# Layer 1 of a convolution front end: two neighbouring positions from five products in place of six

## The chip, the cores and the metric

The kernel runs on one core of one Trainium2 chip. The metric is the device time of one execution in microseconds (us). TensorE (PE in the rows) multiplies, VectorE (DVE), ScalarE (ACT) and GpSimd (POOL) do the elementwise work, SyncE (SP) issues most transfers. Each engine runs its own instructions in order and waits on semaphores for the others.

## The reference, cut to what matters

Eight signals of 120,000 samples go through seven convolutions of 128 channels, each followed by a LayerNorm over the channels and an exact GELU. Four later stages work on the 8 x 374 tokens that are left; the change doesn't touch them.

```python
CONVS = [(128, 10, 5)] + [(128, 3, 2)] * 4 + [(128, 2, 2)] * 2      # channels, taps, stride
for w, g, b, s in zip(conv_ws, ln_gs, ln_bs, strides):
    h = _conv1d(h, w, s)                      # 'VALID', no bias
    h = _fp32_layernorm(swap(h), g, b)        # over the 128 channels
    h = jax.nn.gelu(swap(h), approximate=False)
```

Layer 1 has three taps and stride 2: output position m is w0 x[2m] + w1 x[2m+1] + w2 x[2m+2], where each w is a 128 x 128 matrix. Its outputs m and m+1 both use x[2m+2]: one with w2, the other with w0.

## The kernel before

The samples run through `stream` in 47 chunks (`CHUNKS`, loop variable `j`). A chunk holds 32 positions of layer 0 for 128 stretches of signal, which lie across the partitions. A chunk has eight groups g0 to g7, given by `GROUPS`: g0 to g3 are the four groups of layer 1, g4 is layer 4 (two tiles), g5 is layer 3, g6 and g7 are layer 2. A group is four tiles of 128 x 128 (one bank of PSUM, `psY`), and a tile is three products, one for each tap (`products`, L290). So a layer-1 group is 12 products.

Each group goes round the engines:

- TensorE: `conv` (it waits until the group three before has been normalised, since there are three banks), then the transposes (L299) of the group two before (`LAG = 2`).
- ScalarE: `square` (L349) into `sq`, later `gelu` (L367) of the group two before.
- VectorE: `stats` (the sum L392 into `ss`, and L395, which scales it and adds EPS into `var`), other work of the chunk, then `normalise` (L403).
- GpSimd: `root` (L466), a power of -0.5 over 4 columns, between `stats` and `normalise` of the same group.

Beside that, each chunk makes layer 0 of the next: `window_transposes` and `gram_product` (L323, L329), `patch_squares` (L422, in g0), `patch_stats` (L428 and L430, in g1), `split_patches` (part 0 in g6: L440 to L450; part 1 in g7: L453 to L456), `patch_root` (L472, on GpSimd behind the roots of g2 to g5), `patch_transposes` (L311; the two halves behind g2 and g3 on TensorE) with `copy_patches` (L411; on VectorE between `stats` and `normalise` of g2 and g3), and eight products `layer0` (L339) into `psL`, whose GELU is L383. The second half of `patch_transposes` waits for the copy of the first.

From chunk 8 on, the layers 5 and 6 and the first token stages of a signal (a "side chain" of 36 steps, `pe_chain`, `act_chain`, `dve_chain`, `pool_chain`) are laid over six chunks. `STEP_AT` says behind which of the 48 groups each step goes; -1 is a group without one. On GpSimd, steps 0, 3 and 6 are small roots, 9, 14 and 28 too (L964, L969), 16 and 17 are two additions or products of 125 x 576 (L979, L984), and steps 0, 1 and 3 also issue an indirect DMA each (L989, `pool_scatter`). In the first five chunks VectorE computes tables between the groups instead (`ssm_tables`, L1528 to L1530).

## Time and profile before

| | before |
|---|---|
| median of 3 runs | 2412.24 us (2410.5 to 2412.98) |
| profiled execution | 2409.08 us, span 2407.2 us |
| TensorE busy | 2186.4 us, 91% |
| VectorE busy | 1359.7 us, 56% |
| ScalarE busy | 1141.2 us, 47% |
| GpSimd busy | 861.3 us, 36% |
| products of layers 1 to 4 (L290) | 1045.5 us busy, 8508 rows |

A float32 product of 128 x 128 stands in the profile as two rows (two passes), so 24 rows are the 12 products of a group. The loop over the chunks takes from about 60 us to about 1425 us. One turn of it can be measured by the start of VectorE's copy L416, which comes once in a chunk, ahead of the sum of g6.

### The profile page before, as it was taken

The numbers are of one execution on the slowest core, as the hardware profiler recorded it, in microseconds if no ns is written. First come the engines' busy times: TensorE is split into PE (matmuls) and PEld (weight loads), VectorE is DVE, ScalarE is ACT, GpSimd is POOL, SyncE is SP. The second block draws the span as 40 slices with busy tenths as digits, with TensorE's granted clock in tenths as the row PEclk, the third lists the DMA queues.
The fourth block names the chain that finished last, engine by engine and source line by source line (L and its number), as shares of the span: only waits on it lengthen the run. The fifth ranks groups of instructions, "written<-read, shape, count | busy, mean of one in ns | idle before, by whom it ended". The sixth has DMA issues, their size and how long they took to land. (4 is left out here: it accounts for less than half of the span.)

```text
span 2407.2 us, 45725 instructions
## 1 busy us (share of the span) xinstructions
PE 2186.4 (91%) x16643; PEld 2013.0 (84%) x16643; DVE 1359.7 (56%) x3616; ACT 1141.2 (47%) x2203; POOL 861.3 (36%) x760
## 2 busy tenths in 40 slices
PE   2999999999999999999999995978697899969988
PEld 1999999999999999999999884978465567759988
DVE  4676667667667667667667652422486365542222
ACT  1655565555555565565555541322243465542320
POOL 4444555555555555554554531101330000000000
PEclk9999999999999999999999996999799899989989
DMA  5700000000000000000000202656000010109966
GB/s 159 238 4 4 5 4 4 6 8 4 8 6 4 8 6 4 8 6 4 9 4 1 65 1 73 186 162 181 20 20 1 26 52 39 52 39 326 332 202 223
DMA packets 101336, 150.65 MB, mean 63 GB/s; under 512 B 14692, under 2 KB 79118, under 8 KB 100364
## 3 DMA queue, kind: packets, MB, share of 16 engines
q1 hardware_dynamic: 77580, 118.36, 15.6%
q10 hardware_dynamic: 17984, 20.30, 2.6%
q0 software_dynamic: 5568, 9.27, 1.3%
q8 instruction: 128, 2.10, 0.4%
q14 instruction: 76, 0.62, 0.1%
HBM read 102.32 MB, written 45.50 MB: 61 GB/s over the span
## 5 line engine op out<-in xcount | busy, mean ns | idle before, releaser
L290 PE MATMUL banks<-t_wt,t_l 128*128 128x128 f32 x8508 | 1045.5, 277 | 4.1 <-ACT t_l L367 2.9
L290 PEld LDWEIGHTS banks<-t_wt,t_l 128*128 128x128 f32 x8508 | 1014.9, 193 | 19.5 <-ACT t_l L367 4.1
L466 POOL TENSOR_TENSOR t_rstd<-t_var,t_minus_half 128x4 f32<-128x4 f32 (+1 forms) x379 | 367.0, 968 | 640.1 <-DVE t_var L395 638.7
L349 ACT ACTIVATE t_sq<-banks 128x512 f32<-128x512 f32 (+1 forms) x379 | 216.0, 570 | 523.2 <-PE banks L290 521.3
L403 DVE TENSOR_TENSOR t_yn<-banks,t_rstd 128x512 f32<-128x512 f32 (+1 forms) x379 | 249.1, 657 | 366.2 <-POOL t_rstd L466 364.4
L383 ACT ACTIVATE t_l<-banks,t_cols 128x512 f32<-128x512 f32 x376 | 286.6, 777 | 79.4 <-PE banks L339 76.6
L472 POOL TENSOR_TENSOR t_zrstd<-t_zvar,t_minus_half 128x8 f32<-128x8 f32 x188 | 307.6, 1637 | 25.4 <-DVE t_zvar L430 25.4
L392 DVE TENSOR_REDUCE t_ss<-t_sq 128x4 f32<-128x512 f32 (+1 forms) x379 | 244.7, 646 | 88.8 <-ACT t_sq L349 83.3
L367 ACT ACTIVATE t_l<-banks,t_cols 128x512 f32<-128x512 f32 (+1 forms) x381 | 284.8, 748 | 12.6 <-PE banks L299 7.8
L299 PE MATMUL banks<-t_ident,t_yn 128*128 128x128 f32 x1426 | 220.1, 274 | 13.1 <-DVE t_yn L403 11.9
L299 PEld LDWEIGHTS banks<-t_ident,t_yn 128*128 128x128 f32 x1426 | 173.4, 142 | 27.2 <-DVE t_yn L403 14.9
L339 PE MATMUL banks<-t_p60T,t_w 120*128 120x512 bf16 x376 | 137.4, 386 | 1.9 <-ACT t_l L383 1.8
L1478 POOL TENSOR_TENSOR t_nrstd<-t_nvar,t_minus_half 125x3 f32<-125x3 f32 x24 | 20.7, 863 | 270.1 <-DVE t_nvar L1472 270.1
L1110 ACT ACTIVATE t_G<-banks,t_b1T 128x128 f32<-128x128 f32 x162 | 47.7, 365 | 122.4 <-PE banks L1062 122.0
L2220 DVE TENSOR_SCALAR t_a<-t_H,t_late 128x128 f32 (+1 forms) x128 | 39.3, 340 | 114.9 <-PE banks L2153 106.8
L2152 PE MATMUL banks<-t_a,t_w 128*128 128x128 f32 x384 | 75.7, 279 | 6.5 <-DMA t_w1x<-in_w1x 6.5
L2283 PE MATMUL banks<-t_yb,t_ectb 128*125 128x192 f32 (+1 forms) x384 | 66.5, 336 | 14.0 <-DVE t_yb L2258 10.3
L2283 PEld LDWEIGHTS banks<-t_yb,t_ectb 128*125 128x125 f32 (+1 forms) x384 | 64.9, 194 | 15.6 <-DVE t_yb L2258 10.6
L2086 DVE TENSOR_REDUCE t_ltm<-banks 128x1 f32<-128x374 f32 x64 | 34.8, 544 | 75.5 <-PE banks L1866 75.4
L2153 PE MATMUL banks<-t_a,t_w1x 65*128 65x128 f32 x384 | 75.5, 278 | 0.0
L2160 PE MATMUL banks<-t_w,t_eg 128*128 128x192 f32 x384 | 73.3, 327 | 1.3 <-ACT t_eg L2179 1.3
L395 DVE TENSOR_SCALAR t_var<-t_ss 128x4 f32<-128x4 f32 (+1 forms) x379 | 65.3, 172 | 13.1
(324 smaller groups left out, 3305.5 us busy)
## 6 DMA issues: line engine op xcount, KB each, us to landing
t_w<-in_w SPq DMA_DIRECT2D x64, 480.0 KB
t_w<-in_w SPq DMA_DIRECT2D x27, 576.0 KB, 5.7
ect<-t_ECT SPq DMA_DIRECT2D x16, 750.0 KB, 3.2
t_l<-in_w1a SPq DMA_DIRECT2D x27, 384.0 KB, 5.3
sorted_by_expert<-t_h SPq DMA_DIRECT2D x4, 2400.0 KB, 11.0
routed_by_expert<-t_h SPq DMA_DIRECT2D x4, 2400.0 KB, 17.4
t_ectb<-ect ACTq DMA_DIRECT2D x5, 1500.0 KB, 7.9
t_w1x<-in_w1x SPq DMA_DIRECT2D x64, 97.5 KB
```

The lines of the kernel that those rows point to most:

```text
L290: mm = pe.matmul(psY[bank][:, t * C:(t + 1) * C], src[:, at:at + P], T["wt"][:, 3 * (layer - 1) + k, :], start=(k == 0), stop=(k == 2))
L299: mm = pe.transpose(psT[:, t * P:(t + 1) * P], T["yn"][:, par, t * C:(t + 1) * C], T["ident"][:, :])
L339: pe.matmul(psL[i % 2][:, :], T["w60"][:, slot, :], p60T[:, 4 * q:4 * q + 4, :].rearrange("r a p -> r (a p)"), start=True, stop=True).then ...
L349: act.activation(T["sq"][:, par, 0:n], psY[bank][:, 0:n], ACT.Square).then_inc(S["squared"], 1)
L367: act.activation(dst, psT[:, 0:n].rearrange("c (t p) -> c t p", p=P), ACT.Gelu, bias=T["cols"][:, 8 + layer:9 + layer], scale=T["cols"][:, ...
L383: act.activation(view(T["l0"][:, :], [[2 * BLOCK, 4], [1, P]], block_at(0, 8 * q + slot)), psL[i % 2][:, :].rearrange("c (a p) -> c a p", ...
L392: dve.reduce_sum(T["ss"][:, par, 0:n], T["sq"][:, par, 0:n * C].rearrange("p (t c) -> p t c", c=C), axis=AX.X)\
L403: dve.tensor_tensor(T["yn"][:, par, 0:n * C].rearrange("p (t c) -> p t c", c=C), psY[bank][:, 0:n * C].rearrange("p (t c) -> p t c", c=C), ...
L466: pool.tensor_tensor(T["rstd"][:, par, 0:n], T["var"][:, par, 0:n], T["minus_half"][:, 0:n], ALU.pow)\
L472: pool.tensor_tensor(T["zrstd"][:, s], T["zvar"][:, s], T["minus_half"][:, 0:POS // 4], ALU.pow)\
L2152: pe.matmul(o, T["w12"][:, r, c * P:(c + 1) * P], T["a1"][:, r % RING, :], start=True, stop=False)
L2283: mm = pe.matmul(pO[k % 2][0:n, 0:D], T["ectb"][:, b % MIX_RING, c, t * TOK:t * TOK + n], T["yb"][:, b % MIX_RING, c, :], start=(c == 0), ...
```

## The change

Layer 1 (g0 to g3) is computed as follows. For the pair of outputs m and m+1, which share x[2m+2], one product with `wsum` = w0 + w2 is made of the shared input (the shared product). Each of the two outputs then takes its middle tap as before, and one product of a difference: x[2m] - x[2m+2] with w0, x[2m+4] - x[2m+2] with w2. The shared product is added to both. A group has 2 + 4 + 4 = 10 products.

- TensorE: `pair_products` puts the two shared products into `psL` ahead of the wait for the bank, then the eight others into `psY`.
- GpSimd: `differences` writes 128 x 512 differences into `dif` for each of the four groups: one instruction for three of them, three instructions for the first. They stand ahead of the roots of g6, g7, g0 and g1.
- ScalarE: `read_shared` copies the 128 x 256 shared products from PSUM to `shared`.
- VectorE: `add_shared` adds them to the bank in PSUM. It stands ahead of `normalise` of the group before (of g7 for g0), and waits for the products of its own group. `square` of layer 1 now waits for it.
- VectorE's L395 is gone from the groups: the square is scaled by 1/sqrt(C) on ScalarE, and EPS is a 129th column of `sq`.
- The two halves of `patch_transposes` and `copy_patches` stand one group earlier (g1 and g2), and `STEP_AT` is another table.
- To make room, `v` holds two signals in place of eight, with a wait for the indirect DMA two signals back.

```diff
     def conv(pe, j, g):
-        layer = GROUPS[g][0]
-        pe.wait_ge(S["normed"], count(j, g) - BANKS)
-        if layer == 1:
-            if g == 0:
-                pe.wait_ge(S["l0_ready"], 8 * (j + 1))
+        if g == 0:
+            pe.wait_ge(S["l0_ready"], 8 * (j + 1))
+        if g < WG:
+            pair_products(pe, j, g)
         else:
...
+    def pair_products(pe, j, g):
+        _, half, bank, par, _, _ = event(j, g)
+        if sums(j, g) > 2:
+            pe.wait_ge(S["shared_read"], sums(j, g) - 2)
+        for p in range(2):
+            at = tap(1, out_blocks(1, half)[2 * p], 2)
+            mm = pe.matmul(psL[par][:, p * C:(p + 1) * C], T["l0"][:, at:at + P], T["wsum"][:, :], start=True, stop=True)
+        mm.then_inc(S["shared_done"], 1)
+        pe.wait_ge(S["normed"], count(j, g) - BANKS)
+        pe.wait_ge(S["dif_ready"], 4 * j + (2, 2, 3, 4)[g])
+        for t, m in enumerate(out_blocks(1, half)):
+            o, at = psY[bank][:, t * C:(t + 1) * C], tap(1, m, 1)
+            pe.matmul(o, T["l0"][:, at:at + P], T["wt"][:, 1, :], start=True, stop=False)
+            mm = pe.matmul(o, T["dif"][:, half, t * P:(t + 1) * P], T["wt"][:, t % 2 * 2, :], start=False, stop=True)
+        mm.then_inc(S["conv_done"], 1)
...
-        dve.reduce_sum(T["ss"][:, par, 0:n], T["sq"][:, par, 0:n * C].rearrange("p (t c) -> p t c", c=C), axis=AX.X)\
-            .then_inc(S["summed"], 1)
-        dve.wait_ge(S["summed"], number)
-        dve.tensor_scalar(T["var"][:, par, 0:n], T["ss"][:, par, 0:n], 1.0 / C, EPS, ALU.mult, ALU.add)\
-            .then_inc(S["var_ready"], 1)
+        dve.reduce_sum(T["var"][:, par, 0:n], T["sq"][:, par, 0:n, :], axis=AX.X).then_inc(S["summed"], 1)
+
+    def read_shared(act, j, g):
+        par = event(j, g)[3]
+        act.wait_ge(S["shared_done"], sums(j, g))
+        if sums(j, g) > 2:
+            act.wait_ge(S["added"], sums(j, g) - 2)
+        act.activation(T["shared"][:, par, :], psL[par][:, 0:2 * C], ACT.Copy).then_inc(S["shared_read"], 1)
+
+    def add_shared(dve, j, g):
+        _, _, bank, par, number, _ = event(j, g)
+        shared = view(T["shared"][:, par, :], [[C, 2], [0, 2], [1, C]])
+        y = psY[bank].rearrange("p (a b c) -> p a b c", a=2, b=2)
+        dve.wait_ge(S["shared_read"], sums(j, g))
+        dve.wait_ge(S["conv_done"], number)
+        dve.tensor_tensor(y, y, shared, ALU.add).then_inc(S["added"], 1)
...
+    def differences(pool, j, half):
...
+        pool.wait_ge(S["conv_done"], count(j - 1, 3))
+        pool.wait_ge(S["l0_ready"], 8 * j + (7, 3, 5, 7)[half])
+        if half == 0:
+            at = block_at(0, POS - 2) - 1
+            pool.tensor_tensor(out[:, 0, :], l0[:, at:at + P], even(1, 1)[:, 0, :], ALU.subtract)
+            pool.tensor_tensor(out[:, 1, :], even(2, 1)[:, 0, :], even(1, 1)[:, 0, :], ALU.subtract)
...
+        pool.tensor_tensor(o, pairs, middle, ALU.subtract).then_inc(S["dif_ready"], 1)
...
-    STEP_AT = [-1, 0, 1, -1, 2, 3, 4, -1, 5, 6, 7, 8, 9, 10, 11, 12, -1, 13, 14, 15, -1, 16, 17, 18, -1, 19, 20, 21, 22, 23, -1, 24, 25,
-               -1, 26, 27, 28, 29, 30, 31, -1, 32, 33, -1, 34, 35, -1, -1]
+    STEP_AT = [0, -1, 1, -1, 2, 3, 4, -1, 5, 6, 7, -1, 8, 9, 10, -1, 11, 12, -1, 13, 14, 15, 16, 17, 18, -1, 19, 20, 21, 22, 23, 24, 25,
+               -1, 26, -1, 27, 28, 29, -1, 30, 31, 32, 33, -1, 34, 35, -1]
...
                 for g in range(NG):
+                    if g < 2:
+                        differences(pool, j, g + 2)
+                    if g >= 6 and j + 1 < CHUNKS:
+                        differences(pool, j + 1, 7 - g)
                     root(pool, event(j, g))
```

VectorE from the sum of g7 to the normalise of g0, before (L392 and L395 `stats`, L403 `normalise`, L453 to L456 the second part of `split_patches`, L422 `patch_squares`):

```order
L392 TENSOR_REDUCE t_ss<-t_sq 128x4
L395 TENSOR_SCALAR t_var<-t_ss 128x4
L403 TENSOR_TENSOR t_yn<-banks,t_rstd 128x512
L453 TENSOR_TENSOR t_p<-t_rest,t_p 128x32x10
L455 COPY t_p<-t_p 128x32x10 x2
L456 COPY t_p<-t_p 128x32x10
```

The same place after (L430 `stats`, L445 `add_shared`, L452 `normalise`, L502 to L505 `split_patches`, L471 `patch_squares`), on to the normalise of g0:

```order
L430 TENSOR_REDUCE t_var<-t_sq 128x4
L445 TENSOR_TENSOR banks<-banks,t_shared 128x512
L452 TENSOR_TENSOR t_yn<-banks,t_rstd 128x512
L502 TENSOR_TENSOR t_p<-t_rest,t_p 128x32x10
L504 COPY t_p<-t_p 128x32x10 x2
L505 COPY t_p<-t_p 128x32x10
L430 TENSOR_REDUCE t_var<-t_sq 128x4
L471 TENSOR_TENSOR t_zz<-banks,t_xs 128x320
L445 TENSOR_TENSOR banks<-banks,t_shared 128x512
L452 TENSOR_TENSOR t_yn<-banks,t_rstd 128x512
```

L395 has gone, and the addition for the next group has come between the sum and the normalise.

GpSimd from the last `patch_root` (L540) of a chunk to g2 of the next, after (L515 `root`, L527, L528 and L535 `differences`). Before, only the five roots stand between the two L472:

```order
L540 TENSOR_TENSOR t_zrstd<-t_zvar,t_minus_half 128x8
L535 TENSOR_TENSOR t_dif<-t_l 128x512
L515 TENSOR_TENSOR t_rstd<-t_var,t_minus_half 128x4
L527 TENSOR_TENSOR t_dif<-t_l 128x128
L528 TENSOR_TENSOR t_dif<-t_l 128x128
L535 TENSOR_TENSOR t_dif<-t_l 128x256
L515 TENSOR_TENSOR t_rstd<-t_var,t_minus_half 128x4
L535 TENSOR_TENSOR t_dif<-t_l 128x512
L515 TENSOR_TENSOR t_rstd<-t_var,t_minus_half 128x4
L535 TENSOR_TENSOR t_dif<-t_l 128x512
L515 TENSOR_TENSOR t_rstd<-t_var,t_minus_half 128x4 x2
L540 TENSOR_TENSOR t_zrstd<-t_zvar,t_minus_half 128x8
```

The roots of g6, g7, g0 and g1 now each stand behind the differences of a later group.

## Rows read from the trace of the kernel before

**Rows 1.** Busy time by engine: a chunk without side chain, six with it.

```profile
core 0: us, PE busy (x) PEld busy (x) DVE busy (x) ACT busy (x) POOL busy (x), PEclk, DMA share, GB/s
...
227.99:254.83 26.84, 26.84 (x243) 26.30 (x242) 16.37 (x40) 16.18 (x28) 14.13 (x13) 1.00 0.02 4
...
518.72:695.50 176.78, 175.95 (x1545) 170.64 (x1545) 119.36 (x307) 102.15 (x180) 96.55 (x84) 1.00 0.02 6
```

**Rows 2.** Who TensorE waited for, 60 to 1430 us: sum, times, longest.

```profile
PE banks L525 <- DVE t_yn L718: 7.5, 4, 2.5
PE banks L311 <- DVE t_p60T L411: 6.8, 5, 1.9
```

**Rows 3.** Timeline of TensorE over g0 to g1 of chunk 5: start, length.

```profile
207.35 2.84 PE L290 MATMUL banks<-t_wt,t_l 128*128 128x128 f32 x24
210.03 0.60 PE L299 MATMUL banks<-t_ident,t_yn 128*128 128x128 f32 x4
210.47 2.84 PE L290 MATMUL banks<-t_wt,t_l 128*128 128x128 f32 x24
```

**Rows 4.** Timeline of VectorE: the copy L416 of chunks 1 and 2.

```profile
114.10 0.42 DVE L416 COPY t_xT<-banks 85x256 f32<-85x256 f32 x1
...
142.90 0.42 DVE L416 COPY t_xT<-banks 85x256 f32<-85x256 f32 x1
```

**Rows 5.** Timeline of VectorE: g1 of a chunk, to the sum of g2.

```profile
213.91 0.68 DVE L392 TENSOR_REDUCE t_ss<-t_sq 128x4 f32<-128x512 f32 x1
214.62 0.17 DVE L395 TENSOR_SCALAR t_var<-t_ss 128x4 f32<-128x4 f32 x1
215.91 0.69 DVE L403 TENSOR_TENSOR t_yn<-banks,t_rstd 128x512 f32<-128x512 f32 x1 [1.12 <-POOL t_rstd L466]
216.52 0.48 DVE L428 TENSOR_REDUCE t_zs<-t_zz 128x32 f32<-128x320 f32 x1
...
217.12 0.68 DVE L392 TENSOR_REDUCE t_ss<-t_sq 128x4 f32<-128x512 f32 x1
```

**Rows 6.** Timeline of GpSimd, g2 and g3 of the same chunk.

```profile
218.08 1.01 POOL L466 TENSOR_TENSOR t_rstd<-t_var,t_minus_half 128x4 f32<-128x4 f32 x1 [2.21 <-DVE t_var L395]
219.06 1.64 POOL L472 TENSOR_TENSOR t_zrstd<-t_zvar,t_minus_half 128x8 f32<-128x8 f32 x1
220.69 1.01 POOL L466 TENSOR_TENSOR t_rstd<-t_var,t_minus_half 128x4 f32<-128x4 f32 x1
```

**Rows 7.** Timeline of VectorE: `patch_squares`, and both parts of `split_patches` with what follows.

```profile
204.20 0.48 DVE L440 TENSOR_TENSOR t_scaled<-t_xs,t_zrstd 128x320 f32<-128x320 f32 x1
...
205.85 0.28 DVE L1529 TENSOR_SCALAR t_late<-t_cosT,t_sv 128x118 f32<-128x118 f32 x1
...
209.16 0.48 DVE L453 TENSOR_TENSOR t_p<-t_rest,t_p 128x320 bf16<-128x320 f32 x1
...
210.26 0.16 DVE L1528 TENSOR_TENSOR t_sv<-t_sv 128x1 f32<-128x1 f32 x1 [0.16 <-DVE t_p L456]
...
212.09 0.48 DVE L422 TENSOR_TENSOR t_zz<-banks,t_xs 128x320 f32<-128x320 f32 x1
```

**Rows 8.** Timeline of GpSimd: step 17 of the side chain, ahead of chunk 23.

```profile
726.48 1.41 POOL L984 TENSOR_TENSOR t_h<-t_h,t_late 125x576 f32<-125x576 f32 x1
```

**Rows 9.** Timeline of VectorE at the same time: the first operation of `split_patches`.

```profile
727.15 1.08 DVE L440 TENSOR_TENSOR t_scaled<-t_xs,t_zrstd 128x320 f32<-128x320 f32 x1
```

**Rows 10.** Timeline of GpSimd: step 0 with its indirect DMA, chunk 20.

```profile
651.88 0.85 POOL L964 TENSOR_TENSOR t_rstd<-t_var,t_minus_half 125x3 f32<-125x3 f32 x1 [2.07 <-DVE t_var L708]
652.94 1.28 POOL L989 DMA_INDIRECT sorted_by_expert<-t_v,t_row  x1 [0.21 <-issue]
654.25 1.05 POOL L466 TENSOR_TENSOR t_rstd<-t_var,t_minus_half 128x4 f32<-128x4 f32 x1
```

**Rows 11.** Timeline of VectorE around that step 0.

```profile
651.71 0.68 DVE L392 TENSOR_REDUCE t_ss<-t_sq 128x4 f32<-128x512 f32 x1
...
655.33 0.69 DVE L403 TENSOR_TENSOR t_yn<-banks,t_rstd 128x512 f32<-128x512 f32 x1 [2.14 <-POOL t_rstd L466]
```

More of the change, by code:

```diff
@@ L52 @@
 BANKS = 3
+WG = 4
 XS_RING = 4
@@ L202, in _ @@
                 .then_inc(S["wt_centred"], 1)
+            dve.wait_ge(S["wt_centred"], 1)
+            dve.wait_ge(S["w0_split"], 1)
+            dve.tensor_tensor(T["wsum"][:, :], T["wt"][:, 0, :], T["wt"][:, 2, :], ALU.add)
         @block.tensor
@@ L254, in event, with sums, sums_behind @@
         return GROUPS[g] + ((NG * j + g) % BANKS, g % 2, count(j, g), P * j)
+    def sums(j, g):
+        return WG * j + g + 1
+    def sums_behind(j, g):
+        return (j, g + 1) if g + 1 < WG else (j + 1, 0) if g + 1 == NG and j + 1 < CHUNKS else None
     END = (CHUNKS + 1) * NG
@@ L335, in layer0 @@
             pe.wait_ge(S["patch_copied"], 2 * c + i // 4 + 1)
-        if not isinstance(c, int) or 8 * c + i >= 2:
+        if c >= 1 and i < 2:
+            pe.wait_ge(S["shared_read"], sums(c - 1, 2 + i))
+        if 8 * c + i >= 2:
             pe.wait_ge(S["l0_ready"], 8 * c + i - 1)
@@ L344, in square @@
     def square(act, e):
-        layer, _, bank, par, number, _ = e
+        layer, half, bank, par, number, _ = e
         n = tiles(layer) * C
-        act.wait_ge(S["conv_done"], number)
+        if layer == 1:
+            act.wait_ge(S["added"], sums(number // NG - 1, half))
+        else:
+            act.wait_ge(S["conv_done"], number)
         act.wait_ge(S["summed"], number - 2)
-        act.activation(T["sq"][:, par, 0:n], psY[bank][:, 0:n], ACT.Square).then_inc(S["squared"], 1)
+        act.activation(T["sq"][:, par, 0:tiles(layer), 0:C], psY[bank][:, 0:n].rearrange("p (t c) -> p t c", c=C), ACT.Square,
+                       scale=C ** -0.5).then_inc(S["squared"], 1)
     def gelu(act, e, carry=None):
@@ L467, in root @@
             .then_inc(S["rstd_ready"], 1)
+    def differences(pool, j, half):
+        l0 = T["l0"]
+        even = lambda i, n: view(l0[:, :], [[4 * BLOCK, n], [1, P]], block_at(0, 8 * half - 2 + 2 * i))
+        out = T["dif"][:, half, :].rearrange("p (t c) -> p t c", c=P)
+        pool.wait_ge(S["conv_done"], count(j - 1, 3))
[4 more added lines that the diff above has]
+            pool.tensor_tensor(out[:, 1, :], even(2, 1)[:, 0, :], even(1, 1)[:, 0, :], ALU.subtract)
+            pairs, o = view(l0[:, :], [[4 * BLOCK, 2], [1, P]], block_at(0, 2)), out[:, 2:4, :]
+            middle = view(l0[:, :], [[0, 2], [1, P]], block_at(0, 4))
+        else:
+            pairs = view(l0[:, :], [[4 * BLOCK, 2], [4 * BLOCK, 2], [1, P]], block_at(0, 8 * half - 2))
+            middle = view(l0[:, :], [[4 * BLOCK, 2], [0, 2], [1, P]], block_at(0, 8 * half))
+            o = out.rearrange("p (a b) c -> p a b c", a=2)
+        pool.tensor_tensor(o, pairs, middle, ALU.subtract).then_inc(S["dif_ready"], 1)
     def patch_root(pool, c, part):
@@ L1315, in _ @@
                         gram_product(pe, j + 3)
+                    if g == 1 and j + 1 < CHUNKS:
+                        patch_transposes(pe, j + 1, 0)
                     if g == 2 and j + 1 < CHUNKS:
-                        patch_transposes(pe, j + 1, 0)
-                    if g == 3 and j + 1 < CHUNKS:
                         patch_transposes(pe, j + 1, 1)
@@ L1344, in _ @@
                 gelu0(act, 0, i)
+            read_shared(act, 0, 0)
             for j in range(CHUNKS):
@@ L1359, in _ @@
                     act_chain(act, *chain_at(j, g))
+                    if sums_behind(j, g):
+                        read_shared(act, *sums_behind(j, g))
             gelu(act, event(CHUNKS - 1, 6))
@@ L1396, in _ @@
                 split_patches(dve, c, 1)
+            add_shared(dve, 0, 0)
             for j in range(CHUNKS):
@@ L1403, in _ @@
                         patch_squares(dve, j + 2)
+                    if g == 1 and j + 1 < CHUNKS:
+                        copy_patches(dve, j + 1, 0)
                     if g == 2 and j + 1 < CHUNKS:
-                        copy_patches(dve, j + 1, 0)
-                    if g == 3 and j + 1 < CHUNKS:
                         copy_patches(dve, j + 1, 1)
+                    if sums_behind(j, g):
+                        add_shared(dve, *sums_behind(j, g))
                     normalise(dve, event(j, g))
@@ L1441, in _ @@
                     patch_root(pool, c, part)
+            differences(pool, 0, 1)
+            differences(pool, 0, 0)
             for j in range(CHUNKS):
                 for g in range(NG):
+                    if g < 2:
+                        differences(pool, j, g + 2)
+                    if g >= 6 and j + 1 < CHUNKS:
+                        differences(pool, j + 1, 7 - g)
                     root(pool, event(j, g))
@@ L2421, in program @@
                         sl("w0parts", [TAPS0, 3, C], BF16)
[L2422 removed]
+                        sl("wsum", [P, C])
+                        T["w0rest"] = T["wsum"][0:TAPS0, :]
                         sl("w0c", [P, TAPS0])
@@ L2436, in program @@
                         sl("p60T", [2 * ROWS, PAIRS, P], BF16)
+                        sl("dif", [P, 4, 4 * P])
+                        sl("shared", [P, 2, 2 * C])
                         sl("l0", [P, BLOCK * BLOCKS[0]])
```

32 lines of the change are left out of this document (19 added, 13 removed).

## The prediction

> **What bounds the kernel now.** I read the busy time by engine first, then who TensorE waits for. In the loop over the chunks TensorE is the bound: a chunk without side chain takes 26.84 us and TensorE is busy for all of it, six chunks with side chain take 176.78 us and it is busy for 175.95 [rows 1]. Its waits in the loop come to a handful, 6.8 us for the copied patches and 7.5 for step 1 of the side chain [rows 2]. VectorE is busy for 61% of the plain chunk and GpSimd for 53%, 68% and 55% in the six. That looks like ample room. It isn't, because the two take turns: a group's sum is followed by a root on GpSimd, and the normalise queued behind it on VectorE waits for that root. The first sum starts at 213.91 and the normalise at 215.91, 2.00 us of which VectorE works 0.85; the next operation starts 0.61 later [rows 5]. So I add up the turn of VectorE and GpSimd in order, as if TensorE were always ready, and compare it with TensorE's own sum. I count from the sum of g7 to that of the next g7.
>
> **The turn before.** g7: 2.61, and 1.10 for the second part of the split (209.16 to 210.26) [rows 5, 7]. g0: 2.61. g1: 2.61 and 0.60 for the patch sums (216.52 to 217.12) [rows 5]. g2: 2.61. That is 12.14 to the sum of g3; the copies and squares between sum and normalise hide under the root. The root starts 0.96 after the sum (2.00 less 1.04 for the root and its signal), so at 13.10. From here GpSimd is the path: root 0.98, patch root 1.63, root, and so on [rows 6]; the root of g4 has two columns and takes about 0.66. Root 3, patch root, root 4, patch root, root 5 end at 18.94. The normalise of g5, the window copy and the sum of g6 with its signal give 20.9; root 21.9, normalise 22.6, first part of the split 1.65 (204.20 to 205.85) [rows 7]: 24.2 us. TensorE needs 26.84. The margin is 2.6 us.
>
> As a test of the method: the first five chunks carry the tables of VectorE, about 0.7 us behind most groups, and take 28.8 us (114.10 to 142.90) [rows 4]. The turn plus tables gives 24.2 + 4.6, and TensorE waits. So the turn can be the bound, and is there.
>
> **TensorE after.** Twelve products take 210.03 - 207.35 = 2.68 us, 0.223 each [rows 3]. Ten instead of twelve in four groups: 8 x 0.223 = 1.79 us less, so 25.05 in a plain chunk and 29.46 - 1.79 = 27.67 in one with side chain. Over 47 chunks this is 84 us, what the change could give at most.
>
> **The turn after, part by part.**
> - L395 is gone: its result came 0.25 later than the sum's (214.62 to the root) and the root now follows the sum by some 0.77. Sum to normalise is 1.81, a group 2.42. This saves 0.19 in each group on VectorE's path.
> - add_shared isn't in the trace. It reads PSUM and SBUF over 512 columns and writes PSUM; bounds are 0.48 (L422, 320 columns, the same sources) [rows 7] and 0.69 (L403, 512 columns) [rows 5]. I take the latter, 0.61 to the next operation. In g7 it hides under the root; in g0 with L422 it just fits (1.74 of 1.81); in g1 and g2 with the copy it makes 1.90, so 0.09 each.
> - read_shared is 256 columns on ScalarE, which is busy for 16.18 of 26.84 [rows 1], and has two thirds of the products' time to do it. Nothing.
> - The differences. The nearest row is 125 x 576 on GpSimd, 1.41 us [rows 8]: 512 columns at 2.45 ns are 1.25. The group in three instructions lies between 1.25 and 2.0; I take 1.45. The ones ahead of the root of g6 stand directly in GpSimd's path: +1.25, of which 0.35 fits into the time in which it waited for the sum. The others fit between roots.
> - Their second cost is on VectorE. In the trace one operation of `split_patches` runs while L984 does. L984 lasts from 726.48 to 727.89; L440 starts at 727.15 and takes 1.08 in place of 0.48, ending 0.34 after it [rows 7 to 9]; so in six of six side chains. The differences of the next g0 start right behind the root of g6, exactly as L984 did, so L440 loses about 0.6 in every chunk. Those of g2 start behind the root of g7 and hold L453 for about 0.4. The bounds for both are 0 and 1.5, all of the differences that outlasts the normalise (1.45 - 0.61 and 1.25 - 0.61). I take 1.0, since that is how L440 fared.
>
> The Trainium skill, page SBUF — State Buffer, section "Who interferes with whom", says that a VectorE instruction with two SBUF inputs and a GpSimd instruction that reads SBUF exclude each other for the whole instruction, and whoever starts second waits it out. The trace agrees for L440 (it ended 0.34 after L984). Copies and casts, it says, can take the shared ports too; by that rule the rest of the split would be held as well and the cost would be 1.5 in place of 1.0, 24 us over the loop.
>
> Sum: g7 1.81 + 0.61 + 1.10 + 0.4 = 3.93; g0 2.42; g1 1.90 + 0.61 + 0.60 = 3.11; g2 2.51; sum of g3 at 11.97. Its root would start at 12.75 and GpSimd is free at 12.8. Root, patch root, root, patch root, root, patch root end at 20.3, the differences at 21.5, root 6 at 22.5, normalise 23.2, split 1.65 + 0.6: **25.45 us**. The turn was 2.6 us shorter than TensorE's sum; now it is 0.4 longer. A plain chunk becomes 25.45 in place of 26.84.
>
> **The side chain on top.** It adds (119.36 / 6) - 16.37 = 3.5 us of VectorE and 2.0 of GpSimd to a chunk [rows 1], and on TensorE 2.6. Before, a margin of 2.6 and TensorE's own 2.6 took that up. Now, for six chunks, by the new table: steps of VectorE behind g6, g7, g0, g1 and g2, where nothing hides them, 11.9 us (0.92 for a pair of 374-column products, 1.7 for step 35, and so on). Steps of GpSimd in its path 9.6: step 0 stands at g0, and its small root 0.85 and its indirect DMA 1.28 come ahead of the differences and of the root of g1. In the trace this already stretched 2.00 to 655.33 - 651.71 = 3.62 [rows 10, 11]; now the differences are added, about 2.9 more than the 1.90. Steps 1 and 3 cost 1.3 and 2.1, steps 9, 14 and 28 some 1.1 each. Steps 16, 17 and 25 meet the port as L440 did: 1.6. What spills over in g3 and g4: 2.1. Round trips over TensorE when its part of a step is behind g2: 2.1. Together 27.3 us, 4.55 a chunk. The turn is then 30.0 us, against 27.67 for TensorE and 29.46 measured before. So six chunks take 180.0 in place of 176.78.
>
> **Total.** Five batches of six at +3.3: +16.5. The first batch has no indirect DMAs (4.1 less): -2. The last three chunks have a step behind every group: +3. Five table chunks: 25.45 + 4.6 against 28.8, +6. Three plain ones: 3 x -1.4 = -4. The first differences stand between the last GELU of layer 0 and the first products: +1.5, bounds 0 and 3. Nothing changes behind the loop. Sum +21, which makes 2430 us of the profiled execution's 2409.08. That execution was 3.2 us under the median of the runs, so the median should go from 2412 to about 2433 us.
>
> **Rivals.**
> 1. *The turn is overlapped after all*, since TensorE may be two groups ahead, and TensorE stays the bound. For it: 61% busy. Against it: the table chunks. It gives 2412 - 84 + some 10 us of stalls = 2338. It decides if the turn with side chain is under 27.7.
> 2. *No port cost*: the differences are short, or VectorE slips between them. The turn loses 1.0 a chunk, and 1.6 in a batch: -47 - 10, so 2376. Against it: L440 in six of six.
> 3. *Slower still*: each stall of TensorE comes back. The second patch transposes, behind g2, wait for a copy that now stands behind the sum of g1; TensorE reaches it with nothing to spare, and what follows (0.45 of transposes, 2.23 of products, add_shared) reaches VectorE late. With 0.5 a chunk for the port at its upper bound and 0.3 for these trips: 47 x 0.8 = +38 on the forecast, so 2471.
> 4. *The side chain hides better*: a quarter of its 27.3 us falls into waits that I count as none, among them VectorE's wait for the root in g3 to g5. -6.8 x 6.5 = -44, so 2389. For it: TensorE's waits before are far below what single late groups would suggest [rows 2]. Against it: 3.62 in place of 2.00 [rows 11].
>
> **How the numbers follow.** Forecast 0.45, rival 1 0.12, rival 2 0.12, rival 3 0.17, rival 4 0.14. I predict 2433 us. The range leaves out rival 1 and takes in the others, with the upper bound of the port cost: 2368 to 2472. A measurement of this kernel can tell about 0.2% (5 us). Rivals 1, 2 and 4 are faster, and the forecast loses 0.05 to no change: faster 0.36, same 0.06, slower 0.58.
>
> **What would show it.** TensorE's idle time in the loop goes from some 20 us to over 100, waiting for L460 (the copied patches) and L452 (the normalise). The copy L465 comes every 25.4 to 26 us in chunks 5 to 7 and every 30 on average later. L489 takes about 1.08 in every chunk. The differences take 1.2 to 1.3 us. Chunks with step 0 are the longest. If the copies come every 27.7 us I am wrong about the turn; if L489 takes 0.48, about the port.

## The result, and the profile after

The changed kernel takes **2502.12 us** (median; 2497.45 to 2504.8) against 2412.51 (2410.5 to 2412.98) for the kernel before on the same chip: a ratio of 1.0377, 95% interval 1.0362 to 1.0391. The prediction was 2433 with a range of 2368 to 2472. Slower was right; the 90 us are four times the 21 that were summed up.

Section 1 of the page after (busy time of each engine):

```profile
PE 2152.1 (86%) x15891; PEld 1959.3 (78%) x15891; DVE 1453.5 (58%) x3426; ACT 1193.7 (48%) x2391; POOL 1116.5 (45%) x1043
```

TensorE was busy for 2186.4 us before. It has lost only 34 us of work, GpSimd has gained 255 and VectorE 94, and no engine is near full. One round of VectorE and GpSimd through a chunk's eight groups is the turn of the forecast; the part of it from the sum of one group to that of the next is called a trip here. By the start of the copy that comes once in a chunk (L416 before, L465 after), the 96 us of span lie so:

| stretch | before | after | more | forecast |
|---|---|---|---|---|
| to the fourth of these copies | 84.42 | 86.93 | 2.5 | 1.5 |
| four chunks with tables | 116.8 | 120.5 | 3.7 | 6 (for five) |
| three plain chunks | 80.4 | 82.8 | 2.4 | -4 |
| six chunks, first batch | 178.3 | 186.5 | 8.2 | -2 |
| five batches of six | 884.1 | 943.3 | 59.2 | 16.5 |
| the rest | 1063.2 | 1083.0 | 19.8 | 3 |

The five batches hold most of it, but for its length the worst place is the last three chunks, which stand in "the rest": from the sum of g7 of chunk 43 to that of chunk 46 it is 116.5 us after and 97.2 before. Behind the loop nothing is lost. Of the three plain chunks the first takes 29.11 us (26.73 before), the two others 26.82 and 26.83, as before.

Who TensorE waits for after, 60 to 1500 us (sum, times, longest). L343 is `patch_transposes`, L373 `layer0`, L306 and L307 the products of layer 1 in `pair_products`; L471 is `patch_squares`, L421 the GELU of layer 0, L535 `differences`. It answers to [rows 2]:

```profile
PE banks L343 <- DVE t_zz L471: 56.5, 37, 2.8
PE banks L373 <- ACT t_l L421: 40.9, 44, 2.4
PE banks L306 <- POOL t_dif L535: 30.2, 36, 3.1
```

The same question for VectorE. L452 is `normalise`, L515 `root`, L445 `add_shared`:

```profile
DVE t_yn L452 <- POOL t_rstd L515: 272.9, 222, 3.1
DVE banks L445 <- PE banks L307: 92.3, 63, 7.1
DVE t_var L430 <- ACT t_sq L386: 42.7, 39, 2.7
```

So TensorE, which waited for almost nothing [rows 2], waits 128 us in these three rows, for three different things. VectorE in turn waits 92 us for TensorE: the addition stands in the queue before the products it needs are made. Not all of that is new. Before, VectorE already waited for TensorE's products by way of ScalarE's square, and the last two rows above (135 us) stand against this one, of the kernel before over the same 60 to 1500 us:

```profile
DVE t_ss L392 <- ACT t_sq L349: 83.3, 83, 8.6
```

The windows of the plain chunk, of six chunks with side chain (forecast: 180.0), and of all five batches, with the columns of [rows 1]:

```profile
236.58:263.40 26.82, 25.44 (x227) 24.57 (x226) 18.08 (x35) 17.22 (x33) 19.54 (x19) 1.00 0.02 5
853.82:1043.04 189.22, 170.55 (x1452) 162.63 (x1451) 131.94 (x282) 108.80 (x204) 129.27 (x120) 0.99 0.02 6
476.70:1420.05 943.35, 849.41 (x7243) 809.07 (x7242) 659.62 (x1408) 544.04 (x1015) 646.50 (x596) 0.99 0.02 5
```

In this plain chunk TensorE's work fell nearly as forecast (to 25.44; forecast 25.05), and the chunk took as long as before.

**One turn, row by row.** VectorE from the sum of g7 (269.29) to the sum of g3 (282.06). L430 is the sum, L502 to L505 the second part of `split_patches`, L460 `copy_patches`:

```profile
269.29 0.68 DVE L430 TENSOR_REDUCE t_var<-t_sq 128x4 f32<-128x516 f32 x1
270.75 0.70 DVE L445 TENSOR_TENSOR banks<-banks,t_shared 128x512 f32<-128x512 f32 x1 [0.78 <-PE banks L307]
271.36 0.68 DVE L452 TENSOR_TENSOR t_yn<-banks,t_rstd 128x512 f32<-128x512 f32 x1
...
273.27 0.69 DVE L430 TENSOR_REDUCE t_var<-t_sq 128x4 f32<-128x516 f32 x1 [0.16 <-DVE t_p L505]
273.87 0.48 DVE L471 TENSOR_TENSOR t_zz<-banks,t_xs 128x320 f32<-128x320 f32 x1
274.27 0.69 DVE L445 TENSOR_TENSOR banks<-banks,t_shared 128x512 f32<-128x512 f32 x1
275.08 0.69 DVE L452 TENSOR_TENSOR t_yn<-banks,t_rstd 128x512 f32<-128x512 f32 x1
275.68 0.68 DVE L430 TENSOR_REDUCE t_var<-t_sq 128x4 f32<-128x516 f32 x1
276.28 0.68 DVE L460 COPY t_p60T<-banks 120x1024 bf16<-120x1024 bf16 x1
277.52 0.70 DVE L445 TENSOR_TENSOR banks<-banks,t_shared 128x512 f32<-128x512 f32 x1 [0.56 <-PE banks L307]
278.13 0.68 DVE L452 TENSOR_TENSOR t_yn<-banks,t_rstd 128x512 f32<-128x512 f32 x1
...
279.33 0.68 DVE L430 TENSOR_REDUCE t_var<-t_sq 128x4 f32<-128x516 f32 x1
...
282.06 0.69 DVE L430 TENSOR_REDUCE t_var<-t_sq 128x4 f32<-128x516 f32 x1
```

GpSimd and TensorE at the same time:

```profile
276.44 1.01 POOL L515 TENSOR_TENSOR t_rstd<-t_var,t_minus_half 128x4 f32<-128x4 f32 x1 [0.16 <-DVE t_var L430]
```
```profile
273.15 0.60 PE L331 MATMUL banks<-t_ident,t_yn 128*128 128x128 f32 x4
274.50 0.63 PE L343 MATMUL banks<-t_identb,t_p 128*120 128x128 bf16 x8 [0.75 <-DVE t_zz L471]
274.96 0.66 PE L300 MATMUL banks<-t_wsum,t_l 128*128 128x128 f32 x4
...
277.03 0.39 PE L307 MATMUL banks<-t_wt,t_dif 128*128 128x128 f32 x2
```

From g7 to g0 it took 3.98 us (forecast 3.93), in part by luck: the addition waited 0.78 for its products and put the normalise 2.07 behind the sum in place of 1.81, and the split lost less than was forecast. From g0 to g1 it took 2.41 (2.42). From g1 to g2 it took 3.65 where the forecast had 3.11, and this is why: TensorE came to the patch transposes at 273.75, waited 0.75 for the squares of g0 (273.87 on VectorE), and so finished the products of g2 late, at about 277.4. The addition waited for them 0.56, to 277.52. The root of g1 was ready at 277.45, but its normalise stands behind the addition and ran at 278.13, 0.68 late. A late VectorE makes TensorE late, and through the addition TensorE makes VectorE late: the forecast left the second out.

There is a second place. Behind the sum of g3 the forecast has the roots and patch roots of g3, g4 and g5 back to back. The sum of g5 waited for its square, which waits for products, and GpSimd stood idle before the root of g5:

```profile
287.81 0.69 DVE L430 TENSOR_REDUCE t_var<-t_sq 128x4 f32<-128x516 f32 x1 [1.25 <-ACT t_sq L386]
```
```profile
288.58 1.01 POOL L515 TENSOR_TENSOR t_rstd<-t_var,t_minus_half 128x4 f32<-128x4 f32 x1 [0.88 <-DVE t_var L430]
```

**The trips on the mean.** From the start of one sum to that of the next, mean of the 30 chunks of the five batches, us, in the kernels before and after and in five of the runs below:

| trip | before | after | no differences | no addition | neither | transposes back | squares first |
|---|---|---|---|---|---|---|---|
| g6 to g7 | 4.59 | 6.09 | 4.98 | 6.25 | 5.21 | 6.07 | 6.08 |
| g7 to g0 | 4.12 | 4.36 | 3.85 | 4.34 | 3.78 | 4.36 | 4.77 |
| g0 to g1 | 2.90 | 2.93 | 2.92 | 2.93 | 2.85 | 2.93 | 2.92 |
| g1 to g2 | 3.84 | 4.49 | 4.38 | 3.79 | 3.54 | 3.82 | 3.94 |
| g2 to g3 | 3.81 | 3.66 | 3.65 | 3.34 | 3.31 | 3.48 | 3.67 |
| g3 to g6 | 10.20 | 9.94 | 10.04 | 9.93 | 9.94 | 9.96 | 9.95 |

Against the kernel before, the chunk is longer in two places: from g6 to g7 (1.50), where the differences stand ahead of the root, and from g1 to g2 (0.65).

### The profile page after: what moved, and what is told of

It is laid out like the page before. It is cut to its first block and busy times, and to the rows that moved or that the text cites. A ratio compares the mean times of both kernels' runs of the same rounds, so it can differ in the third digit from the quotient of the medians.

```text
span 2503.0 us, 45303 instructions
## 1 busy us (share of the span) xinstructions
PE 2152.1 (86%) x15891; PEld 1959.3 (78%) x15891; DVE 1453.5 (58%) x3426; ACT 1193.7 (48%) x2391; POOL 1116.5 (45%) x1043
## 5 line engine op out<-in xcount | busy, mean ns | idle before, releaser
L515 POOL TENSOR_TENSOR t_rstd<-t_var,t_minus_half 128x4 f32<-128x4 f32 (+1 forms) x379 | 367.4, 969 | 466.0 <-DVE t_var L430 465.3
L322 PE MATMUL banks<-t_wt,t_l 128*128 128x128 f32 x3996 | 509.4, 278 | 2.9 <-ACT t_l L405 2.9
L322 PEld LDWEIGHTS banks<-t_wt,t_l 128*128 128x128 f32 x3996 | 495.8, 195 | 15.6 <-ACT t_l L405 4.0
L452 DVE TENSOR_TENSOR t_yn<-banks,t_rstd 128x512 f32<-128x512 f32 (+1 forms) x379 | 248.3, 655 | 290.4 <-POOL t_rstd L515 283.1
L306 PE MATMUL banks<-t_wt,t_l 128*128 128x128 f32 x1504 | 303.0, 284 | 33.2 <-POOL t_dif L535 33.1
L540 POOL TENSOR_TENSOR t_zrstd<-t_zvar,t_minus_half 128x8 f32<-128x8 f32 x188 | 307.7, 1638 | 25.4 <-DVE t_zvar L479 25.4
L421 ACT ACTIVATE t_l<-banks,t_cols 128x512 f32<-128x512 f32 x376 | 288.1, 781 | 62.8 <-PE banks L373 59.6
L307 PE MATMUL banks<-t_wt,t_dif 128*128 128x128 f32 x1504 | 300.0, 282 | 0.0
L430 DVE TENSOR_REDUCE t_var<-t_sq 128x4 f32<-128x516 f32 (+1 forms) x379 | 246.2, 650 | 74.2 <-ACT t_sq L386 64.1
L306 PEld LDWEIGHTS banks<-t_wt,t_l 128*128 128x128 f32 x1504 | 237.5, 199 | 39.5 <-issue 39.3
L307 PEld LDWEIGHTS banks<-t_wt,t_dif 128*128 128x128 f32 x1504 | 237.3, 199 | 0.0
L535 POOL TENSOR_TENSOR t_dif<-t_l 128x512 f32<-128x512 f32 (+1 forms) x188 | 224.8, 1196 | 2.5 <-ACT t_l L421 2.1
L445 DVE TENSOR_TENSOR banks<-banks,t_shared 128x512 f32<-128x512 f32 x188 | 130.3, 693 | 107.7 <-PE banks L307 103.2
L373 PE MATMUL banks<-t_p60T,t_w 120*128 120x512 bf16 x376 | 138.2, 388 | 42.0 <-ACT t_l L421 41.9
L300 PE MATMUL banks<-t_wsum,t_l 128*128 128x128 f32 x752 | 122.7, 287 | 1.2 <-ACT t_l L421 1.2
L343 PE MATMUL banks<-t_identb,t_p 128*120 128x128 bf16 x752 | 61.1, 226 | 61.8 <-DVE t_zz L471 57.2
L343 PEld LDWEIGHTS banks<-t_identb,t_p 128*120 128x120 bf16 x752 | 53.2, 138 | 73.9 <-issue 73.2
```

Of the source, the lines that this page charges most:

```text
L306: pe.matmul(o, T["l0"][:, at:at + P], T["wt"][:, 1, :], start=True, stop=False)
L307: mm = pe.matmul(o, T["dif"][:, half, t * P:(t + 1) * P], T["wt"][:, t % 2 * 2, :], start=False, stop=True)
L322: mm = pe.matmul(psY[bank][:, t * C:(t + 1) * C], src[:, at:at + P], T["wt"][:, 3 * (layer - 1) + k, :], start=(k == 0), stop=(k == 2))
L421: act.activation(view(T["l0"][:, :], [[2 * BLOCK, 4], [1, P]], block_at(0, 8 * q + slot)), psL[i % 2][:, :].rearrange("c (a p) -> c a p", ...
L430: dve.reduce_sum(T["var"][:, par, 0:n], T["sq"][:, par, 0:n, :], axis=AX.X).then_inc(S["summed"], 1)
L452: dve.tensor_tensor(T["yn"][:, par, 0:n * C].rearrange("p (t c) -> p t c", c=C), psY[bank][:, 0:n * C].rearrange("p (t c) -> p t c", c=C), ...
```

## The experiments

All were run beside the kernel before; the time is the median, the ratio is against that kernel (its medians in these runs: 2407.2 to 2410.4), and differences of under some 5 us are not told apart. "Five batches" is the stretch of the table above (943.3 after, 884.1 before).

**1. The differences, the addition, both.** In the first edit the subtractions are left out and `dif` holds a constant. The outputs are then not the reference's, nor are they wherever a part of the pair products' arithmetic is left out below.

```diff
...
-        pool.tensor_tensor(o, pairs, middle, ALU.subtract).then_inc(S["dif_ready"], 1)
+        pool.nop().then_inc(S["dif_ready"], 1)
```

> The changed kernel without the subtractions on GpSimd: the buffer of differences keeps a constant, the waits stay. Left out: 4 differences a chunk (1.27 us each). Theory B/C: the time falls by far more than a difference's own place in the order, to 2420 or less, since 5.6 us a chunk of GpSimd time, the port and TensorE's 30 us of waits for them go. Theory A: only the 30 us of waits for the differences go, 2465 to 2475.

Measured: 2425.5 us, ratio 1.0066 (1.0049 to 1.0082); five batches 894.3. The differences cost 77 us, between the two cases of the expectation (2420 or less, and 2465 to 2475). The forecast's terms for them were 0.9 a chunk in GpSimd's path and 1.0 for the port, 47 x 1.9 = 89.

How much of it is the port? Here each difference gives way to powers over six columns, on as little data as a root, one for each group:

```diff
+        pool.tensor_tensor(T["dif"][:, half, 0:6], T["dif"][:, half, 8:14], T["minus_half"][:, 0:6],
+                           ALU.pow).then_inc(S["dif_ready"], 1)
```

> The changed kernel with one power over 6 columns (about 1.3 us on GpSimd, hardly any operand traffic) in place of each group's differences. It keeps GpSimd's time and order and takes away the reading of 512 columns. If VectorE's loss at the shared port matters: 25 to 50 us less than 2502. If GpSimd's time alone matters: within 15 us of 2502 (a little less, since the first group's three subtractions take 1.8 us and the power 1.3).

Measured: 2469.24 us, ratio 1.0249 (1.0229 to 1.0269). 33 us are gone though GpSimd is still taken (a power takes 1.34 us, a difference 1.28, the group in three instructions 1.76; in all GpSimd works 9 us less), and the remaining 44 go when its time is free too. The groups of `split_patches` show where the 33 are. Busy time and mean ns, of after (L502 the add of part 1, L494 the first cast, L489 the first product):

```profile
L502 DVE TENSOR_TENSOR t_p<-t_rest,t_p 128x320 bf16<-128x320 f32 x47 | 44.8, 954 | 0.1
L494 DVE CAST t_p<-t_scaled 128x320 bf16<-128x320 f32 x47 | 31.4, 668 | 1.6
L489 DVE TENSOR_TENSOR t_scaled<-t_xs,t_zrstd 128x320 f32<-128x320 f32 x47 | 27.1, 577 | 6.7 <-POOL t_zrstd L540 6.6
```

and of this experiment (L503, L495, L490 are the same three):

```profile
L503 DVE TENSOR_TENSOR t_p<-t_rest,t_p 128x320 bf16<-128x320 f32 x47 | 22.7, 482 | 0.1
L495 DVE CAST t_p<-t_scaled 128x320 bf16<-128x320 f32 x47 | 15.4, 327 | 1.6
L490 DVE TENSOR_TENSOR t_scaled<-t_xs,t_zrstd 128x320 f32<-128x320 f32 x47 | 26.3, 560 | 6.7 <-POOL t_zrstd L531 6.6
```

The three are 38.9 us longer beside the subtractions, 0.83 a chunk. The forecast had 1.0, with 0.6 on L489, and 1.5 as the upper bound. It fell on the cast: L489 started between two of the short subtractions of g0 and ran in 0.50, and the cast behind it was held by the third. Rows of GpSimd and of VectorE:

```profile
266.54 0.41 POOL L527 TENSOR_TENSOR t_dif<-t_l 128x128 f32<-128x128 f32 x1
266.91 0.46 POOL L528 TENSOR_TENSOR t_dif<-t_l 128x128 f32<-128x128 f32 x1
267.32 0.98 POOL L535 TENSOR_TENSOR t_dif<-t_l 128x256 f32<-128x256 f32 x1
```
```profile
267.21 0.50 DVE L489 TENSOR_TENSOR t_scaled<-t_xs,t_zrstd 128x320 f32<-128x320 f32 x1
267.75 0.74 DVE L494 CAST t_p<-t_scaled 128x320 bf16<-128x320 f32 x1
268.52 0.49 DVE L496 TENSOR_TENSOR t_rest<-t_scaled,t_p 128x320 f32<-128x320 f32 x1
```

The Trainium skill, page SBUF — State Buffer, section "Who interferes with whom", says that casts can take the shared ports as well. The trace agrees: this cast, with one input in SBUF, takes 0.33 us without subtractions beside it and 0.67 with them.

Next, `read_shared` and `add_shared` are left out, and the square waits for the products again:

```diff
-                        add_shared(dve, *sums_behind(j, g))
...
-            act.wait_ge(S["added"], sums(number // NG - 1, half))
+            act.wait_ge(S["conv_done"], number)
```

> The changed kernel without read_shared and add_shared: the shared product is computed and not added, and the square of layer 1 waits for its own products, as before. If the new link (square behind the addition, addition ahead of the normalise) sets the time: 60 us less or more, 2440 or below. If GpSimd's differences and the moved transposes do: within 25 us of 2502.

Measured: 2445.35 us, ratio 1.0149 (1.0132 to 1.0166); five batches 917.6. The addition, with the copy and the waits that belong to it, costs 57 us, again between the two cases (2440 or below, and within 25 of 2502). What the copy on ScalarE has of it was not measured alone. The forecast let it hide under the roots but for 0.09 in g1 and in g2, 8 us in all. The table of trips says where it is: nothing in g7 and g0, 0.70 from g1 to g2 and 0.32 from g2 to g3. The last three chunks alone fall from 116.5 to 100.8 us (without the differences to 105.2). And both left out:

> The changed kernel with neither the subtractions on GpSimd nor the copy and the addition of the shared product; what is left are ten products for twelve, the moved patch transposes, the new step table and the sum without L395. Left out: the differences' values and the shared product's addition. Removing the differences alone gave -77 us, the addition alone -57. If the two costs add: 2502 - 134 = 2368. If they share one path (VectorE waits behind GpSimd either way), 2390 to 2420. If TensorE is the bound again: 2330 to 2345.

Measured: 2360.55 us, ratio 0.9795 (0.9777 to 0.9813). 2502 less 77 and less 57 is 2368, so the two costs nearly add up. What fewer products and the single sum bring with the new order of work is some 50 us against the kernel before (2409.95 beside this run), and the two helpers cost 142.

**2. Is it TensorE's side or the turn?** Here the order, the table and the single sum of after stay, but layer 1 has its twelve products back, no addition, and the differences are computed and not used:

> The changed kernel's order, table and sum, with the 12 products of before and neither copy nor addition of the shared product; GpSimd still computes the differences, and nobody uses them. It does the reference's work. If the differences hide as long as TensorE has its full load: at most 15 us above the kernel before with L395 taken out (2390), so 2390 to 2405. If they stretch the turn whatever TensorE does: 2440 or more.

Measured: 2479.85 us, ratio 1.029 (1.0264 to 1.0316). This run does the reference's work, and the pair products are not needed for a loss. Against the kernel before with one sum (next, 2390.27) it is 90 us. Of that the order and the table may be some 15 (2360.55 to 2345.67, below), though with both helpers in place they cost 55 (experiment 3), so the subtractions' own share is not settled by the times. By trips it stands where they are: g6 to g7 takes 6.25 us here, 5.21 with the same order and no subtractions, 4.26 in the kernel before with one sum. GpSimd's subtractions make the loop longer though no product reads them.

The other way round: the kernel before with one part of the change alone, the scaled square and EPS as the 129th column, so that L395 goes:

```diff
...
-        dve.tensor_scalar(T["var"][:, par, 0:n], T["ss"][:, par, 0:n], 1.0 / C, EPS, ALU.mult, ALU.add)\
-            .then_inc(S["var_ready"], 1)
+        dve.reduce_sum(T["var"][:, par, 0:n], T["sq"][:, par, 0:n, :], axis=AX.X).then_inc(S["summed"], 1)
```

> The kernel before, with only L395 taken out of the groups (the square scaled, EPS as a 129th column). My reading: the turn of VectorE and GpSimd is 1.5 us shorter, which helps only the five table chunks and the few waits: 2 to 10 us less than 2410. Rival (L395 never on the path): no difference.

Measured: **2390.27 us**, ratio 0.992 (0.9906 to 0.9934), 20 us under the kernel before beside it. It computes what the reference does, and beats both kernels. I expected 2 to 10 us. Of its 18.8 us of span, 5.8 are in the four chunks with tables (116.84 to 111.07), where the turn was the bound before, and 7.2 in the five batches, where I took TensorE for the only bound.

**3. The order of the work.** The patch transposes and their copies go back behind g2 and g3:

```diff
-                    if g == 1 and j + 1 < CHUNKS:
+                    if g == 2 and j + 1 < CHUNKS:
                         patch_transposes(pe, j + 1, 0)
-                    if g == 2 and j + 1 < CHUNKS:
+                    if g == 3 and j + 1 < CHUNKS:
                         patch_transposes(pe, j + 1, 1)
```

> The changed kernel with patch_transposes and copy_patches back behind g2 and g3. Theory A (the moved transposes wait for patch_squares, L471, 56.5 us in the trace, and each such wait comes back through the late products and additions): 50 to 90 us less than 2502, that is 2410 to 2450. Theory B (the turn of VectorE and GpSimd is too long wherever the copies stand): within 15 us of 2502, the waits only move to the second half or to layer 0. Theory C (port and order on GpSimd): no change.

Measured: 2466.13 us, ratio 1.023 (1.0213 to 1.0247), between the expected cases once more. The move costs 36 us, which the forecast took as next to nothing: from g1 to g2 the trip falls from 4.49 to 3.82 us, and in the plain chunk from 3.65 to 3.01 (forecast 3.11). It falls to the same 3.01 with the addition out and the transposes where the change puts them, so it takes both to lengthen it. It isn't the main part, though: 54 us of the loss remain. TensorE's waits in the main have other names now:

```profile
PE banks L331 <- ACT t_l L405: 44.9, 33, 2.7
PE banks L306 <- POOL t_dif L535: 36.2, 38, 3.1
```

Then the old `STEP_AT` as well, and after that the old order for the kernel without differences and addition:

> The changed kernel with patch_transposes back behind g2 and g3 and the old STEP_AT, so that only the arithmetic of layer 1 and the sum differ from before. If the new table was part of the cost (step 0 at g0, ahead of the differences of g3): under 2455. If the table fits the new order: over 2475. The version with the transposes back and the new table gave 2466.

Measured: 2446.91 us, ratio 1.0151 (1.0132 to 1.017), 19 us less than with the new table.

> Ten products for twelve and nothing else of the change but the sum without L395: no differences, no addition, patch transposes behind g2 and g3, the old STEP_AT. Left out: the differences' values and the shared product's addition. With the new order and table the same gave 2360.6. If the new order and table cost by themselves: 2320 to 2345, near 2390 - 84 = 2306 for a TensorE that never waits. If the turn is the bound in either order: 2355 to 2370.

Measured: 2345.67 us, ratio 0.9741 (0.9719 to 0.9764). That is 45 us under the kernel before with one sum (experiment 2), and it is what fewer products are worth in this order when nothing is paid for them: about half of the 84 that a count of products promised. TensorE still works for 831 of 844 us of the five batches. This run also keeps the small `v` with its waits, which was never taken out alone.

Is the old table better for itself? With the transposes where the change puts them:

> The changed kernel with the table of steps of the kernel before. With the transposes back at their old places the old table took 19 us less (2447 in place of 2466). If the table is worse for itself, the same 15 to 20 us come here: 2480 to 2487. If the new table is the better one for the new place of the transposes and only misfits the old place, this run takes 2502 or more.

Measured: 2509.81 us, ratio 1.0406 (1.0372 to 1.0441), so not better. The table and the place of the transposes belong together: the old one gives 19 us at the old place, nothing or a small loss at the new.

**4. Single links.** TensorE's largest wait is for the patch squares. In this kernel they go ahead of the sum of g0, first with the transposes at their old place, then in the changed kernel itself:

```diff
+                    if g == 0 and 1 <= j and j + 2 < CHUNKS:
+                        patch_squares(dve, j + 2)
                     stats(dve, event(j, g))
-                    if g == 0 and 1 <= j and j + 2 < CHUNKS:
-                        patch_squares(dve, j + 2)
```

> As the version with the transposes back (2466), with patch_squares ahead of the sum of g0 in place of behind it. There the transposes no longer wait for the squares, so theory A gives no gain, 2460 to 2470; it costs up to 0.4 a chunk (20 us) if the sum of g0 is on the path, as the turn says: 2466 to 2486.

Measured: 2476.31 us, ratio 1.028 (1.0262 to 1.0299), 10 us more than without it: 0.2 a chunk for delaying the sum of g0, which is thus on the path (g7 to g0 is 0.41 longer, the rest a little shorter).

> The changed kernel with one move on VectorE: patch_squares stands ahead of the sum of g0 in place of behind it, so that the first half of patch_transposes (behind g1 on TensorE) finds its squares done. If that link costs time by itself, TensorE's wait for t_zz (56.5 us in all, 37 times) nearly goes and the kernel takes some 20 to 40 us less than 2502, 2462 to 2482. If the turn of VectorE and GpSimd sets the time and the link only shows where its lateness arrives, the squares (0.61 us, 47 times) are put into the turn: the wait moves to the copies of the patches or the normalise, and the time is 2502 to 2531.

Measured: 2498.67 us, ratio 1.0376 (1.0357 to 1.0394): no change. The waits:

```profile
PE banks L343 <- DVE t_zz L471: 34.4, 36, 2.2
PE banks L306 <- POOL t_dif L535: 30.2, 36, 3.1
PE banks L343 <- DVE t_p60T L460: 21.8, 21, 1.8
```

34.4 and 21.8 make 56.2 us at L343, where after the squares had 56.5 and the copy 2.9. TensorE waits there for nearly as long, in part for another semaphore. But the time stayed for another reason too, which the table of trips shows: g1 to g2 became 0.55 shorter (4.49 to 3.94), and g7 to g0 0.41 longer (4.36 to 4.77), since the sum of g0 now stands behind the squares. The link costs what it seems to cost, and this move pays nearly as much for it. The size of a row of waits told neither.

A last suspect was ScalarE, where a GELU (that of the group two before) stands behind a square that now waits for the addition. It goes first, in g0 to g3:

```diff
-                    square(act, event(j, g))
+                    if g >= WG:
+                        square(act, event(j, g))
...
                     gelu(act, event(j - back, (g - LAG) % NG), j - back + (2 if (g - LAG) % NG == 7 else 1))
+                    if g < WG:
+                        square(act, event(j, g))
```

> The changed kernel with ScalarE's order swapped in g0 to g3: the GELU of the group two before ahead of the square. The square waits for the addition, and the GELU behind it holds up the next transposes and layer 0. If this queue on ScalarE is a link of the turn: 25 to 60 us less than 2502. If only VectorE and GpSimd count: within 10 us, or slower, since the square comes up to 0.5 us later.

Measured: 2499.04 us, ratio 1.0365 (1.0332 to 1.0398): no change. TensorE's wait for the GELU of layer 0 fell from 40.9 to 17.1 us, that for the differences rose from 30.2 to 39.4.

> The same swap on the version with the transposes back and the old table (2447), whose trace has 28 us of TensorE waiting for that GELU. Theory of the queue on ScalarE: 2410 to 2430. Otherwise 2440 to 2455. It stays above the kernel before with L395 taken out (2390) either way.

Measured: 2452.91 us, ratio 1.0176 (1.0145 to 1.0207), against 2446.91 without the swap: no gain either. The order of these two on ScalarE is not the cause.

## Why the prediction was right and wrong

- **What bounds the loop.** Right: the turn of VectorE and GpSimd has become the bound, and TensorE waits. Rival 1, the turn overlapped, is refuted by the result, and experiment 2 shows it without any product removed. But the turn is not one of these two alone: TensorE is in it.
- **The differences.** Right in kind and nearly in size. The 512 columns take 1.28 us (1.25 estimated), the group in three instructions 1.76 (1.45). The port took 33 to 39 us in all (47 in the forecast), the time on GpSimd 44 (42). Rival 2, no port cost, is refuted.
- **The addition.** This step failed: "in g1 and g2 with the copy it makes 1.90, so 0.09 each". The addition's own 0.69 us is right, and in g7 and g0 it hides on the mean, as said. But I added up the turn "as if TensorE were always ready", which priced the addition as work and not as a wait. From g1 to g2 it costs 0.70 and from g2 to g3 0.32 in the chunks with side chain, and 57 us in all, where the forecast had 8. In the rows above it waits twice for the products of its own group, and a normalise whose root is ready stands behind it. This is the mechanism of rival 3 with the wrong size and the wrong link: I gave it 0.3 a chunk, 14 us, for a wait for the copied patches, which is 2.9 us in all; the wait is for the squares, one group earlier.
- **The moved transposes.** They are the same failed step: the 0.09 counts what the moved copies do on VectorE. On TensorE the transposes now come one group earlier, close behind the squares and the first copy, and hold up products that VectorE's addition waits for. Measured 36 us; it overlaps with the 57, since in the plain chunk either one taken away brings the trip from g1 to g2 from 3.65 to 3.01.
- **The plain chunk.** 25.45 forecast for one from 236.58, 26.82 measured. From the sum of g7 to that of g3 it is 12.77 in place of 11.97; 0.54 of these 0.80 are the trip from g1 to g2. The other 0.57 come behind the sum of g3, where the root of g5 was 0.88 late for want of its sum, a wait that I took as nothing. The kernel without either helper takes 25.26 on the mean of three, near TensorE's 25.05.
- **The side chain.** 180.0 forecast for six chunks, 189.2 measured. Its own term was right in sum: 4.55 a chunk forecast, and 188.7 / 6 less 26.8 is 4.6 (mean of the five batches). The chunk underneath was 1.4 too short, as in the plain chunk. So rival 4, a side chain that hides better, is refuted. In the last three chunks, with a step behind every group, I had +3 and the runs show +19. Leaving out the addition takes 16 of them back, leaving out the differences 11; which step of the side chain meets which wait stays open.
- **What would show it.** The idle time of TensorE is over 100 us as forecast, but it stands at the squares, the GELU of layer 0 and the differences, not at the copied patches and the normalise. L489 took 0.50 in the chunk shown, which by my own test would have refuted the port cost; the cast behind it and L502 carried it. The copies came every 31.4 us in the five batches, not every 30. The test named one instruction where it should have named the whole split.
- **TensorE's clock** had no place in the forecast (last section).

But for 2.1 us of round trips in a side chain, all terms assumed that nothing goes back from TensorE to VectorE. The terms without such a link came out within a third of their price; the addition came out at seven times its price, and the moved transposes cost 36 us where none but those 8 stood. The range's upper end was rival 3, whose term for these waits was 0.3 a chunk, so the range missed the result for the same reason.

## What to carry to other kernels

When a turn round two engines is added up, list for every new instruction the engine it waits for and what stands behind it in its queue: an instruction that hides by its length doesn't hide if it waits for an engine that the same turn keeps late. Measure it from sum to sum, trip by trip, and not by the largest row of waits. Moving products' work to GpSimd cost twice here, where a root on GpSimd is in the loop: 44 us for its time in the queue and 33 for the shared port under VectorE's SBUF operations. Look first for small work to take off the turn: one instruction of 0.17 us in each group, gone from VectorE, gave 20 us in a kernel whose TensorE showed as full, about half of what two products less in each layer-1 group gave.

## What the runs showed of the hardware

TensorE's granted clock fell after one of its waits. TensorE in one chunk after, around a wait of 2.76 us; then the windows (the figure before the DMA share is the clock):

```profile
992.62 0.63 PE L343 MATMUL banks<-t_identb,t_p 128*120 128x128 bf16 x8 [2.76 <-DVE t_zz L471]
...
993.59 0.40 PE L306 MATMUL banks<-t_wt,t_l 128*128 128x128 f32 x2
993.81 0.61 PE L307 MATMUL banks<-t_wt,t_dif 128*128 128x128 f32 x2
994.21 0.64 PE L306 MATMUL banks<-t_wt,t_l 128*128 128x128 f32 x2
...
996.35 0.63 PE L307 MATMUL banks<-t_wt,t_dif 128*128 128x128 f32 x2
```
```profile
994.00:999.00 5.00, 5.00 (x33) 5.00 (x33) 4.43 (x9) 2.07 (x4) 1.42 (x2) 0.68 0.00 0
1420.05:1516.00 95.95, 74.02 (x568) 70.53 (x567) 50.87 (x131) 44.66 (x84) 51.66 (x55) 0.89 0.15 41
```

The pairs of passes start every 0.43 us in place of 0.22, the lower of the clock's two levels (1.2 against 2.4 GHz), and the products up to 996.77 take twice as long. The clock of 0.68 over these 5 us is a loss of 1.6 us on top of the wait. How much it is in all is less clear. In the five batches the clock is 0.99 (1.00 before); added up over stretches of 4 us, what it lacks comes to 5 us there, to 39 over the loop after, and to 23 over the loop before. So at most some 16 of the 90 us go with the lower clock. TensorE's busy time says nothing surer: it is 849.4 us in the five batches, against 833.3 for the same products in the kernel without either helper, but the last row before a wait counts with its full length (0.60 us for four passes that otherwise are followed after 0.44), and there are three times as many waits. Nor does the sum of the waits decide: without the addition the five batches lack 14 us of clock and TensorE waits 66 us, after 5 and 93. Which waits bring the clock down, no run here shows.
